# Query rows preset by GpSimd instead of ScalarE, query-gate taps as a piece of their own, and maxima in other places around the last experts

## The chip, the cores and the metric

One core of a Trainium2 chip runs the whole program in one launch. The metric is the device time in microseconds (us) from launch to end. The engines are named as the profile names them: PE (TensorE) multiplies, DVE (VectorE) and ACT (ScalarE) work on whole tiles, POOL is GpSimd, and SP only issues DMA transfers here. Each engine runs its own list of instructions in order, and waits on semaphores for the others.

## The reference, cut to what matters

2048 tokens of 128 features pass through four blocks, each added to the residual `x` behind a layer norm.

```
x = x + selective_scan_block(layernorm(x))            # 64 time chunks of 32
x = x + shared_and_8_routed_experts(layernorm(x))     # hidden 512, silu, top 2 of 8
x = x + attention(layernorm(x)):
    q, k = conv3(x), conv3(x) projected;  v = linear(x)          # 16 heads of 8
    tau   = sigmoid(conv1(gelu(depthwise_conv3(x, tau1))))       # one per head and query
    delta = sigmoid(conv1(gelu(depthwise_conv3(x, del1))))       # one per head and key
    scores = (q . k) / sqrt(8) * tau[query] + delta[key]
    x += linear(softmax(scores) @ v)
x = x + hashed_experts(layernorm(x))                  # each token to 2 of 8
```

## The kernel before, in words

The tokens are worked in four chunks of 512. While the scan runs, the routed experts of chunk *tc* run interleaved, and for the last chunk (*tc* = 3) they run by themselves from 642.8 us, in a stretch that also prepares the attention of chunks 0 to 2. The function `scan_order` is called once by every engine, and each engine passes it generators that issue its own part of each named stage; `scan_order` pulls pieces of them in one common order. So moving a call in `scan_order` moves instructions on all engines together.

The experts of a chunk are 9 (one shared, eight routed) times four hidden tiles: 36 *ups* (L631, two matmuls into a hidden tile that ACT turns into `HB` at L1050) and 36 *downs* (L622, two matmuls that sum into one PSUM bank). After an expert's last down, DVE weighs the sum by the token's gate (L1364, `GO`), and the first down of a later expert must wait for that (`gated`); POOL adds it up (L1683). At the end PE turns the sum round (L645), DVE adds it to `x_tok` (L1378), and the layer norm of chunk 3 starts (L1209).

The attention of chunk *c* is prepared by these pieces. `kside`: depthwise taps of the delta gate (DVE, L1425 and L1429), key convolution (PE, L695, `w_convk`), the split of keys into three bf16 parts (DVE L1407 to L1415, `k_parts`), gate product (PE L706, `d2w`), the delta parts on POOL (L1702 to L1710). `qside`: taps of the tau gate (for chunks 0 to 2 on POOL, L1736 to L1742; for chunk 3 on DVE), query convolution (L695, `w_convq`), values (PE L742, DVE L1458), gate product (L706, `t2w`), sigmoid on ACT (L1095), times tau and the split of queries (DVE L1464, then L1407 to L1415, `q_parts`). SP writes the parts to DRAM scratch `sc` (L1905 keys, L1917 delta, L1931 queries) and reads them back as rows: L1912 (12 transfers, keys) and L1922 (6, delta) into the key buffer `KS`, L1896 (12, queries) into `QP`. The rows of query chunk 0 are read when the query parts of chunk 1 are in DRAM.

A score is a product of key rows and query rows. Rows 48 to 50 and 112 to 114 of `QP` meet the three parts of delta, and must be 1. `QP` has two slots; each is filled before its first use, by ACT at L1137, from a column `tmpl` that POOL made at the program's start.

Before the exponentials of a group of heads, the largest score of each query is taken: a pair of matmuls fills two PSUM banks, one DVE reduction of 1024 columns reads them into `mx`. Those of the first head group are split: 16 *early* ones (keys of chunks 0 and 1; PE L779, DVE L1476) run among the last experts, one per scheduling step from step 36 on; 17 *firsts* (keys of chunks 2 and 3; PE L797, DVE L1491) run while chunk 3's attention is prepared; and `AHEAD` = 10 of the second head group (PE L812, DVE L1500) run there too. Then the maxima are reduced (L1487), turned (PE L835), split, and sent through DRAM into `QP`; after that the first score (PE L843) can start the attention proper.

Of the kernel before, what the change touches and what calls it, by code (L numbers as in the profile page):

```python
# [17 lines left out]
NS = 64  # L18
# [56 lines left out]
def scan_order(p):  # L75
# [3 lines left out]
    K0 = p["kside"](0)  # L79
    lgen = chain(some(K0, 4), beside(K0, p["qside"](0)), beside(p["kside"](1), p["qside"](1)), p["later"](2),  # L80
                 beside(p["kside"](2), p["qside"](2)))
    for k in range(-2, NS + 1):
# [36 lines left out]
        if k == NS:  # L119
            lgen = pull(lgen, 2)  # L120
        if 0 <= k - 1 < NS:
# [12 lines left out]
    L, K, Q = p["later"](3), p["kside"](3), p["qside"](3)  # L134
    m = Slots()
# [61 lines left out]
def nothing(*_):  # L197
    pass


PROLOG, NORM, EPILOG, GATES, FFN, COMBINE, KSIDE, QSIDE = 35, 5, 12, 12, 41, 12, 8, 7

IDLE = dict(prolog=lambda tc: idle(PROLOG), epilog=lambda tc: idle(EPILOG), gates=lambda tc: idle(GATES),
            ffn=lambda tc: idle(FFN), later=lambda tc: idle(NORM), combine=lambda: idle(COMBINE), start=nothing,
            kside=lambda c: idle(KSIDE), qside=lambda c: idle(QSIDE), early=nothing, first=nothing, ahead=nothing,
            rows=nothing, mulW=nothing, mulB=nothing, scanX=nothing, scanP=nothing, mulC=nothing, clamp=nothing,
# [127 lines left out]
def build(nc, A, out):  # L334
    with ExitStack() as ctx:
# [595 lines left out]
        def scalar_program(e):  # L931
# [184 lines left out]
            def qside(c):  # L1116
                a, b = RANGE[c]
                yield
                w.wait_ge(S("mm_convq"), c + 1)
                w.wait_ge(S("q_parts"), 5 * c)  # L1120
                conv(c, 0, 0, 1, "conv_q")
                yield
                for g in range(2):
                    if c < 3:
                        w.wait_ge(S("t2"), 10 * c + 5 * g + 5)
                    else:
                        w.wait_ge(S("t1"), 24 + 3 * g + 3)
# [12 lines left out]
                yield  # L1140
                yield
# [54 lines left out]
        def vector_program(e):  # L1196
# [219 lines left out]

            def taps(c, i, g, base):

                a, b = RANGE[c]
                t = TC[2 * i + g][:, 0:b - a]  # L1420
# [4 lines left out]
                e.tensor_scalar(t, xnT[:, a:b], t1w[:, i, g, 0:1], t1w[:, i, g, 3:4], ALU.mult, ALU.add).then_inc(  # L1425
                    S("t1"), 1)
# [18 lines left out]
            def qside(c):  # L1445
                a, b = RANGE[c]
                n = b - a
                if c == 3:
                    w.wait_ge(S("mm_gate_t"), 3)
                    taps(c, 0, 0, 24)  # L1450
                yield
                if c == 3:
                    taps(c, 0, 1, 27)
                yield
                w.wait_ge(S("mm_v"), c + 1)
# [148 lines left out]
        def gpsimd_program(e):  # L1604
# [11 lines left out]

            e.memset(tmpl[:, :], 0.0).then_inc(S("tmpl"), 1)
            for n, p in enumerate((48, 49, 50, 112, 113, 114)):
                w.wait_ge(S("tmpl"), n + 1)
                e.affine_select(out=tmpl[:, :], in_=tmpl[:, :], compare_op=ALU.not_equal, fill=1.0, base=-p,  # L1620
                                pattern=[[0, 1]], channel_multiplier=1).then_inc(S("tmpl"), 1)

            def power(i, st, pre):
# [99 lines left out]

            def qside(c):
                a, b = RANGE[c]
                n = b - a

                def taps(g):
# [23 lines left out]
                if c < 3:
                    taps(1)
                yield
                yield from idle(5)
# [50 lines left out]
        def sync_program(e):  # L1806
# [239 lines left out]
```

## Time and profile before

| | us |
|---|---|
| device time, median of 3 (lowest, highest) | 1692.63 (1691.33, 1693.41) |
| profiled execution, its device time | 1693.37 |
| its span, first to last instruction | 1691.5 |
| last experts: L601 to L645 | 642.80 to 771.27 |
| chunk 3's attention inputs: L645 to L835 | 771.27 to 833.72 |
| first score, L843 | 841.66 |

The mean granted TensorE clock is 0.912. A profile row gives when an instruction (or a run of one form) starts, how long it takes, and in brackets how long its engine stood idle before it and what ended that.

### The profile page before, as it was taken

What the parts mean: (1) busy time and instruction counts of PE and PEld (TensorE: products, weight loads), DVE (VectorE), ACT (ScalarE), POOL (GpSimd) and SP (SyncE); (2) the same over time, 40 slices, a digit from 0 to 9 for tenths busy, and PEclk for the clock granted to TensorE, in tenths of its full rate; (3) what the DMA queues carried; (4) which work ended last, traced back from release to release, by engine and by line L of the source; (5) the groups of instructions that cost most, each with busy time, mean ns of one, the idle gap of its engine ahead of it and who ended that gap; (6) DMA issues with size and microseconds to landing.
All of it is one profiled execution on the core that took longest, in us unless ns stands there. A gap on an engine that the chain in (4) does not pass through costs nothing.

```text
span 1691.5 us, 21904 instructions
## 1 busy us (share of the span) xinstructions
PE 1414.6 (84%) x8188; PEld 515.5 (30%) x8188; DVE 1250.6 (74%) x1498; ACT 1069.8 (63%) x1770; POOL 595.4 (35%) x534
## 2 busy tenths in 40 slices
PE   3445779678966987886499999999999999999998
PEld 1111234233432433332122222222222222344443
DVE  1799888887899783566799999999999994022222
ACT  3532467457725736533189989998999899743433
POOL 0678757865876765452020010001110100000000
PEclk9675789888977988997599999999999999999999
DMA  8122222212222202341112001000100000011110
GB/s 227 38 70 75 64 69 75 69 57 69 87 62 76 81 25 59 62 68 26 40 24 49 27 2 21 2 3 2 21 3 2 2 3 2 26 38 50 44 45 24
DMA packets 57566, 75.59 MB, mean 45 GB/s; under 512 B 7090, under 2 KB 29747, under 8 KB 57459
## 3 DMA queue, kind: packets, MB, share of 16 engines
q1 hardware_dynamic: 57458, 74.18, 16.7%
q8 instruction: 64, 1.05, 0.3%
q14 instruction: 44, 0.35, 0.1%
HBM read 69.18 MB, written 4.98 MB: 44 GB/s over the span
## 4 chain that ended last, share of the span: by engine, by line
PE 51%; DVE 27%; POOL 8%; issue 8%; ACT 4%; DMA 0%; SPq 0%; DVEq 0%; POOLq 0%; ACTq 0%
DVE mx L1500 14%; PE PS L855 11%; PE PS L905 7%; PE PS L917 7%; PE PS L843 6%; PE PS L622 4%; PE PS L812 4%; PE PS L631 4%; POOL D L1655 3%; DVE D L1283 3%; DVE PS L1269 2%; POOL D L1662 2%; DVE PS L1275 2%; PE PS L579 2%; PE PS L547 2%
## 5 line engine op out<-in xcount | busy, mean ns | idle before, releaser
L1168 ACT ACTIVATE aa<-PS 128x512 f32<-128x512 f32 x1024 | 551.3, 598 | 51.0 <-PE PS L843 41.0
L1500 DVE TENSOR_REDUCE mx<-PS 128x2 f32<-128x1024 f32 x480 | 552.2, 1219 | 14.6 <-PE PS L812 11.5
L855 PE MATMUL PS<-aa,D 128*32 128x256 f32 x4096 | 321.6, 391 | 1.6 <-ACT aa L1168 0.6
L843 PE MATMUL PS<-D 54*128 54x512 bf16 x1024 | 212.1, 390 | 15.9 <-ACT aa L1168 8.9
L579 PE MATMUL PS<-D,ident 128*128 128x512 f32 x256 | 155.2, 741 | 64.1 <-POOL D L1662 56.5
L812 PE MATMUL PS<-D 51*128 51x512 bf16 x960 | 190.7, 386 | 17.9 <-DVE mx L1500 16.0
L1766 POOL CAST n<-nm 4x512 bf16<-4x512 f32 x15 | 9.1, 605 | 483.4 <-ACT nm L1150 483.4
L1662 POOL TENSOR_TENSOR D<-D 128x1024 f32<-128x1024 f32 x64 | 150.8, 2356 | 72.2 <-DVE D L1283 72.2
L1189 ACT ACTIVATE D<-PS,h_b 128x512 f32<-128x512 f32 x128 | 88.1, 688 | 130.5 <-PE PS L905 130.5
L1023 ACT ACTIVATE D<-D,Am 128x512 f32<-128x512 f32 x128 | 85.3, 715 | 129.3 <-DVE D L1283 127.4
L1269 DVE TENSOR_TENSOR_SCAN PS<-PS,D 128x512 f32<-128x512 f32 x128 | 157.6, 1231 | 11.3 <-POOL D L1671 3.5
L1655 POOL TENSOR_TENSOR D<-D 128x1024 f32<-128x1024 f32 x64 | 150.6, 2352 | 42.1 <-PE PS L579 37.6
L631 PE MATMUL PS<-xnT,f_w 128*128 128x512 f32 x288 | 152.4, 629 | 13.2 <-ACT HB L1050 13.2
L1050 ACT ACTIVATE HB<-PS 128x512 f32<-128x512 f32 x144 | 85.2, 597 | 107.8 <-PE PS L631 107.4
L622 PE MATMUL PS<-HB,f_w 128*128 128x512 f32 x288 | 150.5, 629 | 1.8 <-ACT FO L1054 1.3
L1588 DVE SCALAR_TENSOR_TENSOR aa<-PS,h_b,aa 128x512 f32<-128x512 f32 x32 | 24.0, 751 | 171.3 <-PE PS L917 171.3
L855 PEld LDWEIGHTS PS<-aa,D 128*32 128x32 f32 x4096 | 84.2, 108 | 194.8 <-issue 154.6
L905 PE MATMUL PS<-xnT,aa 128*128 128x512 f32 x256 | 130.8, 593 | 0.0
L1283 DVE TENSOR_TENSOR_SCAN D<-D,hl,PS 128x512 f32<-128x512 f32 x96 | 122.5, 1276 | 1.9
L843 PEld LDWEIGHTS PS<-D 54*128 54x128 bf16 x1024 | 53.6, 93 | 226.6 <-ACT aa L1168 161.5
L917 PE MATMUL PS<-D 128*128 128x512 f32 x224 | 114.3, 592 | 0.0
L579 PEld LDWEIGHTS PS<-D,ident 128*128 128x128 f32 x256 | 56.9, 235 | 145.7 <-POOL D L1662 74.5
(271 smaller groups left out, 1563.8 us busy)
## 6 DMA issues: line engine op xcount, KB each, us to landing
D<-bc SPq DMA_DIRECT2D x128, 256.0 KB, 3.4
GB<-gd SPq DMA_DIRECT2D x32, 256.0 KB, 3.9
aa<-gh SPq DMA_DIRECT2D x32, 256.0 KB, 3.3
D<-sc SPq DMA_DIRECT2D x72, 64.0 KB
f_w<-in_L_ffn_experts_w SPq DMA_DIRECT2D x1, 2048.0 KB, 9.1
f_w<-in_L_ffn_experts_w SPq DMA_DIRECT2D x8, 256.0 KB, 5.9
aa<-in_L_ffn_W SPq DMA_DIRECT2D x8, 256.0 KB, 3.8
D<-in_L_ffn_W SPq DMA_DIRECT2D x7, 256.0 KB, 4.1
```

What stands on the lines that cost most here:

```text
L579: e.matmul(bank(g), ident[:, :], wb[k % 3][:, g, :], start=(n == 0), stop=(n == 15)).then_inc(S("mm_sum"), 1)
L622: e.matmul(bank(SUM_BANK[tc]), f_w2[:, n // 4, n % 4, :], HB1[i % 6], start=(n % 4 == 0), stop=(n % 4 == 3)).then_inc(S("mm_down"), 1)
L631: e.matmul(bank(4 + i % 2), f_w1[:, n // 4, 128 * (n % 4):128 * (n % 4) + 128], XN[:, ts], start=True, stop=True).then_inc(S("mm_up"), 1)
L812: t = e.matmul(to[:, hh, :], query(hh, qc % 2, p, b), KS[64 * hh:64 * hh + 51, p, 512 * c:512 * c + 512], start=True, stop=True)
L843: e.matmul(take_exp(s + hh), KS[64 * hh:64 * hh + 54, p, 128 * kb:128 * kb + 128], QP[64 * hh:64 * hh + 54, qc % 2, p, :], start=True, sto ...
L855: t = e.matmul(PS[32 * j:32 * j + 32, 7, cs], va[:, kb, 9 * h:9 * h + 32], Pt[K % 3][:, 512 * j + 256 * n:512 * j + 256 * n + 256], start= ...
L905: e.matmul(to, hw1[x % 8][:, 128 * j:128 * j + 128], XN[:, 512 * q:512 * q + 512], start=True, stop=True).then_inc(S("e_full"), 1)
L917: e.matmul(bank(4 + 2 * (x % 2)), hw2[x % 8][:, 128 * j:128 * j + 128], HB3[d % 8], start=(j == 0), stop=(j == 3)).then_inc(S("x_full"), 1)
L1168: e.activation(Pt[K % 3][:, c:c + 512], bank((s + hh) % 3), ACT.Exp).then_inc(S("e_free"), 1)
L1269: e.tensor_tensor_scan(out=bank(3), data0=bank(2), data1=ab[k % 3][:, g, :], initial=0.0, op0=ALU.max, op1=ALU.mult).then_inc(S("sP"), 1)
L1500: e.tensor_reduce(mx4[:, G % 2, b, 2 * pair:2 * pair + 2, c:c + 1], max_banks(m), AX.X, ALU.max).then_inc(freed(m)[0], 1)
L1655: e.tensor_tensor(wb[k % 3], DU[tc % 2][:, :, :], Bb[k % 3].unsqueeze(1).to_broadcast([128, 2, C]), ALU.mult).then_inc(S("wB"), 1)
```

## The change

It has four parts. (1) `QP`'s rows are set to 1 by a POOL memset of the whole slot (128x2048 words of 32 bits) in POOL's `qside`, for chunks 0 and 1; ACT's two fills and the `tmpl` column are gone. (2) The tau gate's taps become a stage `tside` of two pieces, which is on POOL for all four chunks, so DVE's taps of chunk 3 are gone; chunk 3's taps on POOL wait for the key parts. (3) In `scan_order`, `made_beside` puts the pieces of chunks 0 to 2 in another order and at other steps; the early maxima stand at steps 33 to 37, 40 to 43 and 46 to 52 instead of 36 to 51. (4) The order behind the last experts is another, and `AHEAD` is 6 instead of 10: four maxima of the second group now come behind the reduction of the first.

```diff
-    lgen = chain(some(K0, 4), beside(K0, p["qside"](0)), beside(p["kside"](1), p["qside"](1)), p["later"](2),
-                 beside(p["kside"](2), p["qside"](2)))
+    lgen = made_beside(p, K0)
...
     for step, _ in enumerate(chain(p["epilog"](3), both(p["gates"](3), p["ffn"](3)))):
-        if step in (1, 2, 10, 13) or step >= 16:
+        if step in (1, 2, 10, 13):
+            pull(K0)
+        elif step == 8:
+            drain(p["tside"](0))
+        elif step >= 16:
             lgen = pull(lgen)
-        if 0 <= step - EARLY_FROM < EARLY:
-            p["early"](step - EARLY_FROM)
+        if step in EARLY_STEPS:
+            p["early"](EARLY_STEPS.index(step))
...
     pull(K, 4)
+    pull(tau)
+    firsts(3)
+    pull(K, 2)
+    drain(tau)
+    firsts(4)
     pull(Q)
-    pull(K)
-    pull(Q)
-    firsts(3)
-    pull(K)
-    firsts(4)
-    pull(K)
-    pull(Q)
-    firsts(5)
-    pull(Q)
-    firsts(6)
+    firsts(5, 6)
     drain(K)
     pull(Q)
     firsts(7)
-    ahead(0, 1)
     pull(Q)
-    ahead(2, 3)
+    ahead(*range(AHEAD))
+    firsts(8, 9, 10)
+    pull(Q, 2)
+    firsts(11, 12)
     drain(Q)
-    ahead(*range(4, AHEAD))
-    firsts(*range(8, 17))
+    firsts(*range(13, 17))
+
+
+def made_beside(p, K0):
+
+    Q, tau = p["qside"](0), p["tside"](1)
+    yield from beside(K0, some(Q, 4))
+    yield from beside(tau, Q)
+    yield from beside(p["kside"](1), p["qside"](1))
+    yield from p["later"](2)
+    yield from beside(p["kside"](2), chain(p["tside"](2), idle(1), p["qside"](2)))
...
-EARLY, EARLY_FROM = 16, 36
-AHEAD = 10
+EARLY_STEPS = (33, 34, 35, 36, 37, 40, 41, 42, 43, 46, 47, 48, 49, 50, 51, 52)
+AHEAD = 6
...
                 w.wait_ge(S("q_tau"), c)
                 gate(c, tauC, 128, cols[:, 6:7], 1, 0, "gate_t")
-                if c < 2:
-                    w.wait_ge(S("tmpl"), 7)
-                    w.wait_ge(S("mm_sum"), 2 * NS)
-                    e.activation(QP[:, c, :, :], tmpl[:, :].unsqueeze(2).to_broadcast([128, 8, 512]),
-                                 ACT.Copy).then_inc(S("q_tmpl"), 1)
...
-                if c == 3:
-                    w.wait_ge(S("mm_gate_t"), 3)
-                    taps(c, 0, 0, 24)
...
+                    if c == 3:
+                        w.wait_ge(S("k_parts"), 20)
...
+                if c < 2:
+                    e.memset(QP[:, c, :, :].bitcast(mybir.dt.uint32), 0x3F803F80).then_inc(S("q_ones"), 1)
```

Three places of it. The first is PE among the last experts, in two pieces that begin at the same down product (the fourth of expert 4, counted from 0). In the kernel before, L622 is a down, L631 an up, L508 a transpose for chunk 2's norm, L695 the convolutions of chunk 2, L742 its values, L779 the early maximum:

```order
L622 MATMUL PS<-HB,f_w 128x512
L508 MATMUL PS<-ident,xn 128x128 [waits gate_t,p_xn]
L508 MATMUL PS<-ident,xn 128x128 x3
L631 MATMUL PS<-xnT,f_w 128x512 [waits hid]
L695 MATMUL PS<-xnT,w_convk 128x512 [waits gate_d,p_ln]
L695 MATMUL PS<-xnT,w_convk 128x512 x2
L695 MATMUL PS<-xnT,w_convq 128x512 x3
L631 MATMUL PS<-xnT,f_w 128x512 [waits hid]
L622 MATMUL PS<-HB,f_w 128x512 [waits gated]
L622 MATMUL PS<-HB,f_w 128x512
L742 MATMUL PS<-w_Wv,xnT 128x128 x4
L631 MATMUL PS<-xnT,f_w 128x512 [waits hid]
```
Behind these stands one more L622, and then the first L779. In the changed kernel the same down is L632, an up is L641, and the early maximum is L789:

```order
L632 MATMUL PS<-HB,f_w 128x512
L789 MATMUL PS<-D 128x511 [waits d_key1,d_key0,d_q0]
L789 MATMUL PS<-D 128x511
L641 MATMUL PS<-xnT,f_w 128x512 [waits hid]
L789 MATMUL PS<-D 128x512 [waits f_free]
L789 MATMUL PS<-D 128x512
L641 MATMUL PS<-xnT,f_w 128x512 [waits hid]
L632 MATMUL PS<-HB,f_w 128x512 [waits gated]
L632 MATMUL PS<-HB,f_w 128x512
L518 MATMUL PS<-ident,xn 128x128 [waits gate_t,p_xn]
L518 MATMUL PS<-ident,xn 128x128 x3
L789 MATMUL PS<-D 128x511 [waits f_free]
```

The first early maximum now stands directly behind that down; the transpose, the two convolutions, the values, three ups and three downs of the list before stand behind it, and its wait is the same.

The second is DVE behind the query parts of chunk 0, also among the last experts. Before, with L1364 the weighing of expert 1 and L1425, L1429 the delta taps of chunk 1:

```order
L1411 CAST D<-D 128x511 [waits q_parts]
L1413 TENSOR_TENSOR D<-D 128x511 [waits q_parts]
L1415 CAST D<-D 128x511 [waits q_parts]
L1425 TENSOR_SCALAR D<-xnT,t1w 128x512 [waits p_ln,mm_gate_d]
L1429 SCALAR_TENSOR_TENSOR D<-xnT,t1w,D 128x512 [waits t1] x2
L1364 SCALAR_TENSOR_TENSOR GO<-PS,GB 128x512 [waits ffn_sum,d_G0,mm_down]
```

Now, where L1366 is the weighing:

```order
L1413 CAST D<-D 128x511 [waits q_parts]
L1415 TENSOR_TENSOR D<-D 128x511 [waits q_parts]
L1417 CAST D<-D 128x511 [waits q_parts]
L1366 SCALAR_TENSOR_TENSOR GO<-PS,GB 128x512 [waits ffn_sum,d_G0,mm_down]
L1427 TENSOR_SCALAR D<-xnT,t1w 128x512 [waits p_ln,mm_gate_d]
L1431 SCALAR_TENSOR_TENSOR D<-xnT,t1w,D 128x512 [waits t1] x2
```

The weighing moved ahead of the taps, and stays behind the parts.

The third is DVE behind the key parts of chunk 3. Before, L1425 and L1429 are the tau taps of chunk 3, L1491 firsts, L1500 maxima ahead:

```order
L1425 TENSOR_SCALAR D<-xnT,t1w 128x513 [waits mm_gate_t]
L1429 SCALAR_TENSOR_TENSOR D<-xnT,t1w,D 128x513 [waits t1] x2
L1425 TENSOR_SCALAR D<-xnT,t1w 128x513
L1429 SCALAR_TENSOR_TENSOR D<-xnT,t1w,D 128x513 [waits t1] x2
L1491 TENSOR_REDUCE mx<-PS 128x2 [waits m_full] x2
L1458 TENSOR_TENSOR D<-PS,bb 128x16x8 [waits va,mm_v]
L1458 TENSOR_TENSOR D<-PS,bb 128x16x8 x3
L1491 TENSOR_REDUCE mx<-PS 128x2 [waits m_full] x3
L1500 TENSOR_REDUCE mx<-PS 128x2 [waits m_full] x2
L1464 SCALAR_TENSOR_TENSOR D<-D 128x513 [waits gate_t,conv_q]
L1407 CAST D<-D 128x513 [waits d_sq,q_tau]
L1409 TENSOR_TENSOR D<-D 128x513 [waits q_parts]
```

Now, L1487 firsts, L1496 maxima ahead, L1454 values, L1460 to L1417 the query parts:

```order
L1487 TENSOR_REDUCE mx<-PS 128x2 [waits m_full] x5
L1454 TENSOR_TENSOR D<-PS,bb 128x16x8 [waits va,mm_v]
L1454 TENSOR_TENSOR D<-PS,bb 128x16x8 x3
L1496 TENSOR_REDUCE mx<-PS 128x2 [waits m_full] x6
L1487 TENSOR_REDUCE mx<-PS 128x2 [waits m_full] x5
L1460 SCALAR_TENSOR_TENSOR D<-D 128x513 [waits gate_t,conv_q]
L1409 CAST D<-D 128x513 [waits d_sq,q_tau]
L1411 TENSOR_TENSOR D<-D 128x513 [waits q_parts]
L1413 CAST D<-D 128x513 [waits q_parts]
L1415 TENSOR_TENSOR D<-D 128x513 [waits q_parts]
L1417 CAST D<-D 128x513 [waits q_parts]
L1487 TENSOR_REDUCE mx<-PS 128x2 [waits m_full] x3
```

The taps are gone from it. Ahead of the values stand 5 maxima instead of 2, between them and the query parts 11 instead of 5, behind the parts 3 instead of 16: in all 19 instead of 23. On PE the gate product `t2w` of chunk 3, which stood behind the pair for the 3rd of these maxima, now stands behind the pair for the 14th, and three of that 14 wait for `d_key3`.

## Rows read from the trace of the kernel before

**Rows 1.** The page's first part: busy us, share of the span and instructions of each engine.

```profile
PE 1414.6 (84%) x8188; PEld 515.5 (30%) x8188; DVE 1250.6 (74%) x1498; ACT 1069.8 (63%) x1770; POOL 595.4 (35%) x534
```

**Rows 2.** Windows by stage: busy us, instructions; granted TensorE clock, DMA share, GB/s.

```profile
642.80:771.27 128.47, 107.38 (x263) 43.55 (x263) 69.49 (x103) 64.18 (x84) 66.62 (x59) 0.91 0.33 57
771.27:833.72 62.45, 33.67 (x128) 12.07 (x129) 49.17 (x68) 13.04 (x21) 7.67 (x9) 0.64 0.14 27
700.00:708.00 8.00, 5.70 (x8) 2.42 (x9) 3.40 (x7) 3.58 (x6) 1.62 (x2) 0.57 0.66 82
708.00:727.00 19.00, 19.00 (x54) 8.72 (x52) 12.89 (x18) 7.75 (x16) 12.46 (x12) 1.00 0.60 96
```

**Rows 3.** Groups of PE's instructions by line, 708 to 727 us: busy, mean ns, idle.

```profile
L622 PE MATMUL PS<-HB,f_w 128*128 128x512 f32 x16 | 7.8, 592 | 0.0
L631 PE MATMUL PS<-xnT,f_w 128*128 128x512 f32 x14 | 7.0, 592 | 0.0
L695 PE MATMUL PS<-xnT,w_convk 128*128 128x512 f32 x6 | 2.8, 608 | 0.0
```

**Rows 4.** Timeline of PE, 664 to 716 us: start, duration, idle before.

```profile
673.85 2.07 PE L631 MATMUL PS<-xnT,f_w 128*128 128x512 f32 x2 [3.72 <-ACT HB L1050]
...
690.79 1.99 PE L706 MATMUL PS<-D,t2w 128*128 128x512 f32 x4 [0.53 <-DVE D L1458]
...
702.30 2.07 PE L631 MATMUL PS<-xnT,f_w 128*128 128x512 f32 x2 [4.37 <-ACT HB L1050]
...
714.39 1.02 PE L622 MATMUL PS<-HB,f_w 128*128 128x512 f32 x2
```

**Rows 5.** By source line (L1137, L1411, L1716; L1931's landing): duration ns min/median/max, starts.

```profile
L1137 ACT ACTIVATE D<-tmpl x2: 3599/3603/3607, 668.3 to 696.7; 128x4096 bf16<-128x4096 f32 x2
...
L1411 DVE CAST D<-D x8: 430/664/3037, 633.7 to 813.4; 128x512 bf16<-128x512 f32 x4, 128x511 bf16<-128x511 f32 x2, 128x513 bf16<-128x513 f32 x2
...
L1716 POOL MEMSET D<- x4: 1805/1805/1809, 630.6 to 777.9; 128x2048 uint32 x4
...
DMA to landing us min/median/max: 2.6/5.1/7.9
```

**Rows 6.** Timeline of DVE, 664 to 704 us.

```profile
677.28 0.69 DVE L1364 SCALAR_TENSOR_TENSOR GO<-PS,GB 128x512 f32<-128x512 f32 x1 [1.98 <-PE PS L622]
...
696.94 0.73 DVE L1464 SCALAR_TENSOR_TENSOR D<-D 128x512 f32<-128x512 f32 x1 [1.72 <-ACT D L1095]
```

**Rows 7.** Timeline of SP's DMA issues, 700 to 727 us.

```profile
702.72 0.39 SPq L1931 DMA_DIRECT2D sc<-D  x1
710.59 4.10 SPq L1896 DMA_DIRECT2D D<-sc  x12
...
715.13 3.84 SPq L1922 DMA_DIRECT2D D<-sc  x6
```

**Rows 8.** Window of 2 us, in which the last early rows land.

```profile
726.00:728.00 2.00, 2.00 (x7) 0.65 (x6) 1.93 (x3) 1.66 (x2) 1.91 (x2) 1.00 0.21 56
```

**Rows 9.** Timeline of PE, 726 to 768 us: first early maximum, last down products.

```profile
727.07 0.39 PE L779 MATMUL PS<-D 51*128 51x511 bf16 x2
...
765.61 1.98 PE L622 MATMUL PS<-HB,f_w 128*128 128x512 f32 x4
```

**Rows 10.** Timeline of DVE, 770 to 834 us.

```profile
775.33 0.86 DVE L1209 BATCH_NORM_STATS2 st<-x_tok 128x6 f32<-128x128 f32 x4
...
801.03 2.36 DVE L1491 TENSOR_REDUCE mx<-PS 128x2 f32<-128x1024 f32 x2 [6.04 <-PE PS L797]
...
823.96 9.14 DVE L1491 TENSOR_REDUCE mx<-PS 128x2 f32<-128x1024 f32 x8
```

**Rows 11.** Timeline of PE, 786 to 842 us.

```profile
790.59 3.60 PE L706 MATMUL PS<-D,d2w 128*16 128x512 f32 x4 [3.40 <-ACT D L1107]
...
804.23 1.99 PE L706 MATMUL PS<-D,t2w 128*128 128x512 f32 x4 [1.53 <-DVE D L1458]
...
841.66 0.61 PE L843 MATMUL PS<-D 54*128 54x512 bf16 x2 [6.93 <-DMA D<-sc]
```

More of the change, by code:

```diff
@@ L119, in scan_order @@
         if k == NS:
-            lgen = pull(lgen, 2)
+            pull(K0, 2)
         if 0 <= k - 1 < NS:
@@ L128, in scan_order @@
     for step, _ in enumerate(chain(p["epilog"](3), both(p["gates"](3), p["ffn"](3)))):
-        if step in (1, 2, 10, 13) or step >= 16:
+        if step in (1, 2, 10, 13):
[3 more added lines that the diff above has]
+        elif step >= 16:
             lgen = pull(lgen)
-        if 0 <= step - EARLY_FROM < EARLY:
-            p["early"](step - EARLY_FROM)
+        if step in EARLY_STEPS:
+            p["early"](EARLY_STEPS.index(step))
     drain(lgen)
-    L, K, Q = p["later"](3), p["kside"](3), p["qside"](3)
+    L, K, tau, Q = p["later"](3), p["kside"](3), p["tside"](3), p["qside"](3)
     m = Slots()
@@ L198, in nothing @@
     pass
-PROLOG, NORM, EPILOG, GATES, FFN, COMBINE, KSIDE, QSIDE = 35, 5, 12, 12, 41, 12, 8, 7
+PROLOG, NORM, EPILOG, GATES, FFN, COMBINE, KSIDE, TSIDE, QSIDE = 35, 5, 12, 12, 41, 12, 8, 2, 7
 IDLE = dict(prolog=lambda tc: idle(PROLOG), epilog=lambda tc: idle(EPILOG), gates=lambda tc: idle(GATES),
             ffn=lambda tc: idle(FFN), later=lambda tc: idle(NORM), combine=lambda: idle(COMBINE), start=nothing,
-            kside=lambda c: idle(KSIDE), qside=lambda c: idle(QSIDE), early=nothing, first=nothing, ahead=nothing,
+            kside=lambda c: idle(KSIDE), tside=lambda c: idle(TSIDE), qside=lambda c: idle(QSIDE), early=nothing, first=nothing, ahead=nothing,
             rows=nothing, mulW=nothing, mulB=nothing, scanX=nothing, scanP=nothing, mulC=nothing, clamp=nothing,
@@ L215 @@
 LAG = 3
-EARLY, EARLY_FROM = 16, 36
-AHEAD = 10
+EARLY_STEPS = (33, 34, 35, 36, 37, 40, 41, 42, 43, 46, 47, 48, 49, 50, 51, 52)
+EARLY = len(EARLY_STEPS)
+AHEAD = 6
 FIRST = 17 + AHEAD
@@ L364, in build @@
         bb = sb("bb", [128, 2, 128])
-        tmpl = sb("tmpl", [128, 1])
         mx4 = sb("mx4", [128, 2, 4, 4, 5])
@@ L1415, in parts_of, with taps @@
                 e.tensor_copy(out_[2], src).then_inc(done, 1)
-            def taps(c, i, g, base):
+            def taps(c, g):
                 a, b = RANGE[c]
-                t = TC[2 * i + g][:, 0:b - a]
+                t, base = TC[2 + g][:, 0:b - a], 6 * c + 3 * g
                 w.wait_ge(S("mm_out"), 3)
@@ L1424, in taps @@
                 w.wait_ge(S("edge"), 2)
[L1425 removed]
+                e.tensor_scalar(t, xnT[:, a:b], t1w[:, 1, g, 0:1], t1w[:, 1, g, 3:4], ALU.mult, ALU.add).then_inc(
                     S("t1"), 1)
@@ L1434, in kside @@
                 w.wait_ge(S("mm_gate_d"), c)
-                taps(c, 1, 0, 6 * c)
+                taps(c, 0)
                 yield
-                taps(c, 1, 1, 6 * c + 3)
+                taps(c, 1)
                 yield
@@ L1447, in qside @@
                 n = b - a
-                if c == 3:
-                    w.wait_ge(S("mm_gate_t"), 3)
-                    taps(c, 0, 0, 24)
[L1451 to L1454, printed above, removed]
+                yield from idle(2)
                 w.wait_ge(S("mm_v"), c + 1)
@@ L1615, in gpsimd_program @@
             e.memset(starts[:, 0:C:32], E20).then_inc(S("const"), 1)
[L1617 to L1621, printed above, removed]
             def power(i, st, pre):
@@ L1722, in kside, with tside @@
                 yield from idle(2)
-            def qside(c):
+            def tside(c):
                 a, b = RANGE[c]
@@ L1742, in taps, with qside @@
                         e.tensor_tensor(t, t, m, ALU.add).then_inc(S("t2"), 1)
+                taps(0)
+                yield
+                taps(1)
+                yield
+            def qside(c):
                 v = va[:, 4 * c:4 * c + 4, :]
@@ L1748, in qside @@
                 e.memset(v[:, :, 0:144].rearrange("p b (h c) -> p b h c", c=9)[:, :, :, 8:9], 1.0).then_inc(S("va"), 1)
-                if c < 3:
-                    taps(0)
+                if c < 2:
+                    e.memset(QP[:, c, :, :].bitcast(mybir.dt.uint32), 0x3F803F80).then_inc(S("q_ones"), 1)
                 yield
[L1752 to L1755, printed above, removed]
+                yield from idle(6)
             scan_order(IDLE | dict(start=start, prolog=prolog, mulB=mulB, mulC=mulC, clamp=clamp, epilog=epilog, ffn=ffn, later=later,
-                                   kside=kside, qside=qside))
+                                   kside=kside, tside=tside, qside=qside))
             meet(e, w, "pool")
@@ L1890, in load_q @@
                 w.wait_ge(S("d_sq"), 16 * min(qc + 2, 4))
-                w.wait_ge(S("q_tmpl"), sl + 1)
+                w.wait_ge(S("q_ones"), sl + 1)
                 if qc >= 2:
```

7 lines of the change are left out of this document (2 added, 5 removed).

## The prediction, made before the changed kernel ran

> **What bounds the kernel now.** I read the page's first part, then the windows by stage, then the timelines of the engines that wait. PE is busy for 84% of the span, DVE for 74% [rows 1]: neither is the bound everywhere, so the change is worth what the stage is worth in which it lies. All of it lies ahead of the first score. During the last experts PE is busy for 107.38 of 128.47 us [rows 2]: PE's list sets the end there, and what counts is where it stops. It stops twice for ACT: 3.72 us before 673.85 and 4.37 us before 702.30 [rows 4], each time released by the silu of a hidden tile (L1050), because ACT was in L1137, 3.60 us each [rows 5]. After the second stop PE runs at a granted clock of 0.57 for 8 us, and at 1.00 from 708 on [rows 2]: near the lower of its two levels, 1.2 GHz, after an idle stretch, then the upper, 2.4. In the stretch behind (771.27 to 833.72) PE has 33.67 us of work and DVE 49.17 of 62.45 [rows 2], and its last 9.14 us are eight maxima back to back [rows 10]: DVE sets that end, with one hole of 6.04 us before 801.03 [rows 10], where PE is slow with chunk 3's products. From 833.72 to 841.66 little but a trip through DRAM happens: PE idles 6.93 us for it [rows 11].
>
> **The copies (gain).** Without L1137 the two stops go: 2 x 3.60. With them goes slow running: in 700 to 708 PE's busy 5.70 us at 0.57 would be 5.70 x 0.57 = 3.2, so 2.4 less; after the first stop a pair took 2.07 instead of 1.02 [rows 4] and the next one about half of that excess more, 1.6 together. Sum 11.2 us up to the down product that ends at 714.39 + 0.86 = 715.25 (the next instruction's start; 1.02 holds a drain). The POOL memset that replaces a copy takes, by the same size, 1.80 [rows 5]; POOL is busy for 66.62 of 128.47 us [rows 2], and the rows are read by SP only when the query parts of chunk 1 have landed, so I cost it at nothing; were it in front of those parts' own work it would cost 1.8. Building `tmpl` at the program's start lay beside the loads: nothing.
>
> **What PE now waits for instead (loss).** I walked through the new order with the old durations. (a) The weighing of expert 1 stood between taps on DVE and ran at 677.28 [rows 6]; it still stands behind the query parts of chunk 0, which now begin later, since chunk 0's tau product moved back by several products. I get these parts from 671.4 to 676.7, the weighing to 677.5, while PE asks for it at 674.2: 3.3 us. (b) The delta product of chunk 1 is reached 1.6 us before its input. (c) The weighing of expert 3 costs 2.4 us behind the query parts of chunk 1. So PE ends the down of 715.25 at 715.25 - 11.2 + 7.3 = 711.3, some 4 us earlier.
>
> **The first early maximum (the term that decides).** It now stands directly behind that down. Before, the transposes, two convolutions, the values, three ups and three downs stood between, and it ran at 727.07 without idle time [rows 9]. It waits for the rows of query chunk 0, which SP reads when the query parts of chunk 1 lie in DRAM. Before: t2w of chunk 1 at 690.79 [rows 4], parts from 696.94 [rows 6], write issued at 702.72, 12 reads from 710.59, 6 delta reads from 715.13 to 719 [rows 7]; in 726 to 728 the DMA share is down to 0.21 from 0.60 before 727 [rows 2, 8], and the last of these rows lands at 726.9, just in time. None of this chain got shorter but for ACT's copy, which stood behind the sigmoids and so delayed nothing in it. The convolutions of chunk 1 come two downs later, and t2w of chunk 1 ends 1.7 us later by my walk; the parts are done at 704.2 instead of 702.7. From there 24.2 us (702.72 to 726.9) give 728.4; if the write lands in the median of 5.1 us instead of 7.9 [rows 5], 725.6. I take 726.5. PE, there at 711.3, idles for 15 us.
>
> **From there to the norm.** Left on PE are 14 ups, 16 downs, 13 early pairs, the transposes, two convolutions, the values and two gate products. A 512-column product is worth 0.43: in 708 to 727 PE never idles, and 16 + 14 + 12 of them with the short ones fill 19.00 us [rows 2, 3]. So 60 x 0.43 = 25.8, early pairs 13 x 0.32 = 4.2, convolutions 5.2, gates 3.4, the rest 1.3: 39.9. Add slow running after so long a stop, 2.9 (the 2.4 above or a little more), and two shorter waits of my walk, 3.1 (expert 5's gate) and 2.6 (t2w of chunk 2). The last down ends at 726.5 + 39.9 + 2.9 + 5.7 = 775.0, before at 767.53 (765.61 + 1.92) [rows 9]. From there the norm of chunk 3 began 7.8 us later, at 775.33 [rows 10]; now two more early maxima stand on DVE in that tail, 1.0 each net: 9.8. So the norm begins at 784.8: **+9.5**.
>
> **Behind the last experts.** Before, from the norm to 833.72 (L835): 58.4. Up to the key parts nothing changes (15.6). Behind them DVE has 19 maxima at 1.13 (9.14 / 8 [rows 10]) = 21.5, the values 0.9, query parts 3.5, small ones 1.0: 26.9. Holes: the delta product d2w, 3.60 at low clock from 790.59 [rows 11], delays the first maximum by 4.2; the query convolution (3.8) makes a hole of 3.4; key rows of chunk 3 0.8; and t2w, now between two maxima pairs, 3.2, if the clock is low then as it was at d2w (at 804.23 it took 1.99 [rows 11]; then 1.5). 15.6 + 26.9 + 11.6 = 54.1: **-4.3**. Taking the taps from DVE is worth nothing by itself: they filled the hole that ended at 801.03. Most of it is the four maxima, 4.5, which now lie in the gap behind L835. There the fourth's pair stands ahead of the score on PE, and its buffer comes free some 7 us behind L835, when the score could start: 0 to 0.6.
>
> The Trainium skill, "SBUF — State Buffer", section "SBUF: two separate sides", says that VectorE and GpSimd share one pair of ports under an exclusive lock, so that one instruction fully blocks the other. The rows agree in one place: of eight casts at L1411, which take 0.43 us at least and 0.66 in the median, one took 3.04 [rows 5], and it lay beside a POOL memset of 1.80. By that rule new memsets can delay parts; what it would give here is rival 3.
>
> **Sum.** Against the profiled execution's 1693.37 (span 1691.5 and 1.9 around it): +9.5 - 4.3 + 0.3 = 1698.9. The profiled execution is 0.7 above the median of 1692.63, so 1698.2; I shade it to **1697.8**, since a row can land earlier but not much later.
>
> **Rivals.** A measurement of this kernel tells 0.2% (3.4 us) from no change.
> 1. The rows come early enough, so it is faster. The point from which it decides: the sum is zero when they land at 726.5 - 5.5 = 721. For it: a write of this kind landed in 2.6 us at best [rows 5], which from 728.4 gives 723; for more, t2w of chunk 1 must come earlier too. Faster by 0.2% needs 718. With no stop at all (711.3) 15 us of idling and 2.9 of slow running go: 1680. Against it: t2w comes later, not earlier. 0.17.
> 2. Rows at 719 to 723, or a t2w of chunk 3 at full clock: within 0.2%, about 1693. 0.24.
> 3. As forecast, and a new memset on POOL meets a cast of the query parts on DVE, as one met a cast before (3.04 - 0.43 = 2.6 us [rows 5]), or the clock falls in the stops of 3.3 and 3.1 us (it fell after 3.72 us before [rows 4], costing 1.6): 2 to 5 us more, 1701. What delays the parts of chunk 1 delays the landing in full. 0.12.
> 4. The forecast, 1694 to 1700. 0.47.
>
> **How the numbers follow.** Range 1687 to 1703: above it only both mishaps of rival 3, below it rival 1 with landing before 717. Faster 0.17, same 0.24, slower 0.59.
>
> **What would show it.** In the changed trace: L1137 gone and no stop of PE for L1050 near 673 and 702; a weighing at 677 with PE idle for about 3 us; PE idle for 12 to 16 us in front of the first early maximum (L789), which starts between 724 and 729, with the granted clock near 0.5 behind it; L645 at about 778 and the norm (L1211) at 785; from there to L845 about 54 us, with holes on DVE at d2w, w_convq and t2w; the first score 8 us behind. I am wrong if L789 finds its rows landed; then the walk misjudged either PE's arrival or the transfers.

## The result, and the profile after

| | before | changed |
|---|---|---|
| device time, median (lowest, highest), 4 runs each | 1693.02 (1691.33, 1694.06) | 1704.87 (1702.15, 1708.03) |
| profiled execution, its span | 1693.37, 1691.5 | 1708.03, 1706.2 |
| last experts, gate logits to fold (L601 to L645; now L611 to L655) | 128.47 | 139.32 |
| fold to the norm of chunk 3 (L1209; L1211) | 4.06 | 6.22 |
| norm to the turn of the maxima (L835; L845) | 58.39 | 58.62 |
| turn to the first score (L843; L853) | 7.94 | 7.98 |
| all behind it | 849.84 | 849.96 |

The change makes the kernel slower: ratio 1.0072, 95% interval 1.0052 to 1.0091, some 12 us. The profiled execution is the slowest of the four and 14.7 us of span above that of before: 10.9 among the last experts, 2.2 in the tail to the norm, 0.2 in the stretch behind, and 1.3 ahead of all this, where the scan still runs (over the twelve kernels of this study the last experts start anywhere from 640.68 to 644.10 us, and at 642.23 in experiment 4, which is the same program up to there, so this part is scatter).

The windows of the changed kernel, first the last experts, then norm to turn; the columns are those of [rows 2]:

```profile
644.10:783.42 139.32, 109.43 (x260) 43.77 (x261) 66.20 (x102) 62.88 (x86) 70.79 (x62) 0.88 0.26 51
789.64:848.26 58.62, 31.88 (x112) 12.09 (x113) 37.95 (x56) 13.14 (x21) 19.86 (x19) 0.62 0.15 29
679.00:683.00 4.00, 4.00 (x5) 1.84 (x6) 3.89 (x5) 0.00 (x0) 3.79 (x3) 0.50 0.60 164
728.00:732.00 4.00, 4.00 (x8) 1.41 (x7) 3.11 (x4) 1.92 (x5) 1.26 (x1) 0.50 0.10 36
746.00:750.00 4.00, 3.80 (x5) 1.14 (x6) 3.90 (x5) 2.29 (x3) 3.82 (x4) 0.57 0.00 0
```

The last three rows are short pieces of the first window, in which the granted clock is 0.50, 0.50 and 0.57. PE has nearly the same work as before in the first window, which is 10.9 us longer, at 0.88 of full clock instead of 0.91. PE's timeline among the last experts shows where:

```profile
679.00 3.78 PE L632 MATMUL PS<-HB,f_w 128*128 128x512 f32 x4 [3.31 <-DVE GO L1366]
682.57 3.93 PE L705 MATMUL PS<-xnT,w_convk 128*128 128x512 f32 x6
...
695.69 1.89 PE L716 MATMUL PS<-D,d2w 128*16 128x512 f32 x4 [1.43 <-ACT D L1117]
...
710.03 1.98 PE L632 MATMUL PS<-HB,f_w 128*128 128x512 f32 x4 [2.53 <-DVE GO L1366]
...
714.43 1.02 PE L632 MATMUL PS<-HB,f_w 128*128 128x512 f32 x2
727.43 0.61 PE L789 MATMUL PS<-D 51*128 51x511 bf16 x2 [11.98 <-DMA D<-sc]
727.97 2.07 PE L641 MATMUL PS<-xnT,f_w 128*128 128x512 f32 x2
...
746.20 3.63 PE L632 MATMUL PS<-HB,f_w 128*128 128x512 f32 x4 [2.03 <-DVE GO L1366]
...
762.96 3.26 PE L716 MATMUL PS<-D,t2w 128*128 128x512 f32 x4 [2.30 <-issue]
...
783.42 0.63 PE L655 MATMUL PS<-ident,FO 128*128 128x128 f32 x4 [1.63 <-POOL FO L1673]
```

The two stops for the silu behind a copy [rows 4] are gone, and so is L1137. In their place stand a stop of 3.31 us for a weighing of DVE (`GO`), 1.43 for chunk 1's delta gate, 2.53 for a weighing, and 11.98 us for the rows of the first early maximum (L789), which is released by a DMA. In these 11.98 us no instruction of DVE, ACT or POOL runs either. Behind the first of the four stops, four downs take 3.78 us (1.88 at full clock) and the key convolution 3.93 (2.74); behind the fourth, a pair takes 2.07. SP's DMA issues show the chain that L789 waits for, as [rows 7] before:

```profile
709.41 0.39 SPq L1926 DMA_DIRECT2D sc<-D  x1
712.48 4.10 SPq L1891 DMA_DIRECT2D D<-sc  x12
716.62 3.84 SPq L1917 DMA_DIRECT2D D<-sc  x6
```

The write of the query parts (L1926) is issued at 709.41 instead of 702.72, and 18.0 us later L789 starts: the first read is issued 3.1 us behind the write, SP issues the 18 reads one behind the other until 720.46, and 7.0 us more pass before L789 starts. In the stretch behind, DVE's timeline has a hole that before did not have:

```profile
789.64 0.86 DVE L1211 BATCH_NORM_STATS2 st<-x_tok 128x6 f32<-128x128 f32 x4
...
809.53 2.36 DVE L1487 TENSOR_REDUCE mx<-PS 128x2 f32<-128x1024 f32 x2 [3.93 <-PE PS L807]
814.29 3.49 DVE L1487 TENSOR_REDUCE mx<-PS 128x2 f32<-128x1024 f32 x3 [2.40 <-PE PS L807]
824.03 0.88 DVE L1454 TENSOR_TENSOR D<-PS,bb 128x128 f32<-128x128 f32 x4 [6.25 <-POOL D L1746]
...
838.43 2.36 DVE L1487 TENSOR_REDUCE mx<-PS 128x2 f32<-128x1024 f32 x2 [3.34 <-PE PS L807]
```

The values of chunk 3 (L1454) start after 6.25 us of idling, released by POOL's L1746. POOL's timeline shows what it did until then: it waited for the key parts (L1417), then worked through the first piece of the taps, the parts of delta and the second piece of the taps, five operations a piece, and only then through the two memsets of the values' buffer.

```profile
805.81 0.77 POOL L1728 TENSOR_SCALAR D<-xnT,t1w 128x513 f32<-128x513 f32 x1 [11.80 <-DVE D L1417]
...
812.25 0.61 POOL L1692 CAST D<-D 16x513 bf16<-16x513 f32 x1
...
816.60 0.76 POOL L1728 TENSOR_SCALAR D<-xnT,t1w 128x513 f32<-128x513 f32 x1
...
821.97 1.09 POOL L1734 TENSOR_TENSOR D<-D 128x513 f32<-128x513 f32 x1
823.00 0.66 POOL L1744 MEMSET D<- 128x672 f32 x1
823.72 0.21 POOL L1746 MEMSET D<- 128x64 f32 x1
```

In the kernel before, where chunk 3's tau taps were on DVE, POOL set this buffer long before DVE wrote the values at 803.30:

```profile
779.63 0.67 POOL L1746 MEMSET D<- 128x672 f32 x1
780.35 0.21 POOL L1748 MEMSET D<- 128x64 f32 x1
```

In the changed kernel PE is stopped behind DVE, since both buffers of the maxima are full; the last hole of DVE above, 3.34 us, stands behind the gate product `t2w` at 3.78 us:

```profile
826.10 0.60 PE L822 MATMUL PS<-D 51*128 51x512 bf16 x2 [7.88 <-DVE mx L1496]
...
833.43 3.78 PE L716 MATMUL PS<-D,t2w 128*128 128x512 f32 x4
...
848.26 1.01 PE L845 MATMUL PS<-ident,mxh 128*4 128x128 f32 x4 [1.32 <-DVEq L486]
...
856.24 0.61 PE L853 MATMUL PS<-D 54*128 54x512 bf16 x2 [0.47 <-DMA D<-sc]
```

### The profile page after: what moved, and what is told of

It reads as the page before. It is cut to its first block, busy times and chain, and to the rows that moved or that the text cites. A ratio compares the mean times of both kernels' runs of the same rounds, so it can differ in the third digit from the quotient of the medians.

```text
span 1706.2 us, 21900 instructions
## 1 busy us (share of the span) xinstructions
PE 1421.0 (83%) x8188; PEld 516.1 (30%) x8188; DVE 1244.7 (73%) x1492; ACT 1067.7 (63%) x1772; POOL 610.7 (36%) x539
## 3 DMA queue, kind: packets, MB, share of 16 engines
q1 hardware_dynamic: 57458, 74.18, 16.9%
## 4 chain that ended last, share of the span: by engine, by line
PE 51%; DVE 26%; POOL 10%; issue 9%; ACT 3%; DMA 1%; SPq 1%; POOLq 0%; DVEq 0%; ACTq 0%
DVE mx L1496 13%; PE PS L865 11%; PE PS L915 6%; PE PS L927 6%; PE PS L853 6%; PE PS L632 4%; PE PS L822 4%; POOL D L1645 3%; PE PS L641 3%; DVE D L1285 3%; DVE PS L1271 2%; POOL D L1652 2%; PE PS L589 2%; PE PS L557 2%; DVE PS L1277 2%
## 5 line engine op out<-in xcount | busy, mean ns | idle before, releaser
L1496 DVE TENSOR_REDUCE mx<-PS 128x2 f32<-128x1024 f32 x480 | 552.2, 1216 | 10.3 <-PE PS L822 7.1
L853 PE MATMUL PS<-D 54*128 54x512 bf16 x1024 | 212.1, 390 | 9.5 <-ACT aa L1170 8.9
L632 PE MATMUL PS<-HB,f_w 128*128 128x512 f32 x288 | 152.7, 637 | 9.1 <-DVE GO L1366 7.9
L641 PE MATMUL PS<-xnT,f_w 128*128 128x512 f32 x288 | 153.0, 633 | 6.0 <-ACT HB L1060 6.0
L853 PEld LDWEIGHTS PS<-D 54*128 54x128 bf16 x1024 | 53.6, 93 | 220.2 <-ACT aa L1170 161.6
```

The source lines that it names most:

```text
L632: e.matmul(bank(SUM_BANK[tc]), f_w2[:, n // 4, n % 4, :], HB1[i % 6], start=(n % 4 == 0), stop=(n % 4 == 3)).then_inc(S("mm_down"), 1)
L641: e.matmul(bank(4 + i % 2), f_w1[:, n // 4, 128 * (n % 4):128 * (n % 4) + 128], XN[:, ts], start=True, stop=True).then_inc(S("mm_up"), 1)
L853: e.matmul(take_exp(s + hh), KS[64 * hh:64 * hh + 54, p, 128 * kb:128 * kb + 128], QP[64 * hh:64 * hh + 54, qc % 2, p, :], start=True, sto ...
L1496: e.tensor_reduce(mx4[:, G % 2, b, 2 * pair:2 * pair + 2, c:c + 1], max_banks(m), AX.X, ALU.max).then_inc(freed(m)[0], 1)
```

## The experiments

Times are medians. Experiments 1 to 4, 5 to 8, and 9 and 10 ran on three chips, each time with the kernel before beside them (1693.44, 1693.05 and 1693.98). Single executions of one kernel lie several us apart, so the ratio to the kernel before and its interval decide. A difference between two experiments of different groups is the less certain for it. The stage times are those of one profiled execution each.

| kernel | us | ratio, 95% interval | last experts | tail | norm to turn | stop for the first rows |
|---|---|---|---|---|---|---|
| before | 1693.02 | 1 | 128.47 | 4.06 | 58.39 | none |
| changed | 1704.87 | 1.0072 (1.0052, 1.0091) | 139.32 | 6.22 | 58.62 | 11.98 |
| 1 changed, values' buffer first | 1698.31 | 1.0036 (1.0021, 1.0051) | 136.37 | 6.68 | 51.32 | 12.68 |
| 2 changed, taps on DVE | 1699.41 | 1.0032 (1.0018, 1.0046) | 139.27 | 6.22 | 54.47 | 11.96 |
| 3 before, preset alone | 1685.41 | 0.9948 (0.9932, 0.9964) | 117.55 | 4.07 | 61.21 | none |
| 4 changed, early maxima at 37 to 52 | 1691.75 | 0.9992 (0.9983, 1.0002) | 123.30 | 6.68 | 57.59 | none |
| 5 before, six maxima ahead | 1688.30 | 0.9973 (0.9963, 0.9982) | 128.43 | 4.07 | 53.88 | none |
| 6 both repairs of 1 and 4 | 1685.32 | 0.9954 (0.9937, 0.9970) | 123.94 | 6.68 | 54.24 | 0.93 |
| 7 as 3, early maxima at 33 to 52 | 1697.39 | 1.0020 (1.0006, 1.0035) | 128.31 | 6.00 | 60.09 | 13.42 |
| 8 order of before, then the changed one | 1680.92 | 0.9928 (0.9908, 0.9948) | 121.11 | 4.07 | 52.16 | 4.02 |
| 9 as 8, early maxima one step later | 1678.65 | 0.9907 (0.9890, 0.9924) | 117.64 | 6.00 | 53.88 | none |
| 10 as 6, query pieces one step later | 1686.87 | 0.9961 (0.9940, 0.9981) | 125.34 | 6.00 | 52.46 | 1.45 |

**1. The values' buffer ahead of the taps.** In POOL's list for chunk 3:

```diff
             def tside(c):
+                if c == 3:
+                    ones_of_v(c)          # the two memsets of va, moved out of qside
                 taps(0)
```

> The changed kernel, with the memset of chunk 3's values buffer moved ahead of chunk 3's tau taps on GpSimd. In the changed kernel VectorE stood idle for 6.25 us until GpSimd had set that buffer. Theory A (only this wait cost time there): about 6 us less than the changed kernel's 1704.9, so 1699. Theory B (the taps on GpSimd also hold up the delta parts, so that key rows of chunk 3, read from 821.9 on and landed some 7 us later, are late next): the maxima of chunk 3's keys, which would be reached near 824, wait until about 828, and 2 to 3 us are left of the gain, 1702.

Norm to turn fell by 7.3 us, to 51.32, and the time by 6.6: theory A, on the upper side. The DVE hole at the values is gone, and no late key rows took its place. Its trace also serves as a control on the clock:

```profile
726.95 0.61 PE L789 MATMUL PS<-D 51*128 51x511 bf16 x2 [12.68 <-DMA D<-sc]
...
745.37 1.98 PE L632 MATMUL PS<-HB,f_w 128*128 128x512 f32 x4 [2.03 <-DVE GO L1366]
...
760.47 1.96 PE L716 MATMUL PS<-D,t2w 128*128 128x512 f32 x4 [2.30 <-issue]
```

The downs behind the stop of 2.03 us, 3.63 us in the changed kernel, take 1.98 here (granted clock 1.00 from 745 to 749), and the gate product 1.96 instead of 3.26: the same stops, with the clock fallen in one execution and not in the other. It is 3.6 us of the distance from L789 to the fold: 55.99 us with PE busy for 48.70 in the changed kernel, 52.39 with 45.09 here, and 7.3 of idling in both. In experiment 2, where this stage is the same too, the clock fell as in the changed kernel (3.63 and 3.26).

**2. Chunk 3's taps on DVE again**, all else as changed:

```diff
+            def tside(c):                 # DVE; GpSimd's tside passes chunk 3 by
+                if c == 3:
+                    w.wait_ge(S("mm_gate_t"), 3)
+                    taps(c, 0, 0, 24)
```

> The changed kernel, with chunk 3's tau taps back on VectorE, all else as changed. Theory B (GpSimd's taps cost twice, by the values buffer and by late key rows): from the norm of chunk 3 to the turn of the maxima 51 to 54 us instead of 58.6, and 5 to 7 us less than the changed kernel, 1698 to 1700. Rival: the taps' 4.2 us on VectorE come on top of the maxima, and nothing is gained, 1704.

54.47 us from norm to turn and 5.5 us less in all: the wait for the buffer is what the taps on POOL cost, for without them it is gone too. Whether the taps are better on POOL or on DVE once the buffer is first is not shown: the window is 51.32 us in experiment 1 and 54.47 here, but 54.24 in experiment 6, which has this stage as in 1, and the ratios of experiments 1 and 2 can't be told apart.

**3. The preset alone.** The kernel before with ScalarE's copies and `tmpl` out and

```diff
                 if c < 3:
                     taps(1)
+                if c < 2:
+                    e.memset(QP[:, c, :, :].bitcast(mybir.dt.uint32), 0x3F803F80).then_inc(S("q_ones"), 1)
```

> The kernel before, with only the first part of the change: GpSimd presets the query rows, ScalarE's two copies and the column they read are gone. Theory A (the early maxima, not the copies, set the pace from there on): TensorE reaches the first early maximum near 716 instead of 727, and its rows land near 722, since the first copy lay ahead of their chain and the second did not; 5 us are won there, 2 of them lost to a low clock, 1688 to 1690. Rival (what two copies cost is won in full): 11 us less, 1682.

Both theories missed the total, the rival was nearer in the mechanism. PE found the rows there when it came, 73.3 us behind the gate logits instead of 84.3:

```profile
714.74 0.39 PE L778 MATMUL PS<-D 51*128 51x511 bf16 x2
```

```profile
696.08 0.39 SPq L1921 DMA_DIRECT2D sc<-D  x1
700.51 4.11 SPq L1886 DMA_DIRECT2D D<-sc  x12
...
705.06 3.83 SPq L1912 DMA_DIRECT2D D<-sc  x6
```

The last experts are 10.9 us shorter, which is what two copies with their slow clock were put at (11.2), so nothing was lost to the landing: it took at most 18.7 us from the write's issue, not 24.2. Of this 2.8 us went again between norm and turn, where PE was busy for 35.58 us at a granted clock of 0.58; in the kernel before the same window has 32.11 at 0.65:

```profile
763.10:824.31 61.21, 35.58 (x120) 12.73 (x121) 46.20 (x66) 13.02 (x21) 7.66 (x9) 0.58 0.12 28
```

The gate product `t2w` alone took 3.78 us there instead of 1.99 [rows 11]. So the total is 8 us.

**4. The early maxima later, in the changed kernel.**

```diff
-EARLY_STEPS = (33, 34, 35, 36, 37, 40, 41, 42, 43, 46, 47, 48, 49, 50, 51, 52)
+EARLY_STEPS = tuple(range(37, 53))
```

> The changed kernel, with the 16 early maxima at steps 37 to 52, so that the first stands four steps later. Theory A (the stop of 12 us at the first early maximum and the low clock behind it are what the last experts lost): TensorE comes there as the rows land, the stop is 0 to 3 us, and 10 to 14 us less than the changed kernel, 1691 to 1695. Rival (TensorE waits elsewhere instead, for the gates of experts behind a dense run of maxima on VectorE): 1700 or more.

13.1 us less: theory A. L789 starts at 723.34 with no stop, and the last experts take 123.30 instead of 139.32. (That is 16.0 us; the changed kernel's profiled execution is 3.2 us above its median, this one 2.4 below.)

**5. Six maxima ahead, in the kernel before** (`AHEAD = 6`).

> The kernel before, with AHEAD at 6 instead of 10 and nothing else. Theory A (the four maxima lay on VectorE's path at 1.13 us each, and behind the turn of the maxima they fit into the gap of 8 us): 4 us less than the kernel before, 1689. Rival (they come back one for one, in the gap or in the attention): 1693.

4.7 us less, 4.5 of it between norm and turn (53.88); the gap behind is 7.95, as before. Theory A.

**6. Both repairs of the changed kernel.**

> The changed kernel, with the values buffer set ahead of the tau taps and the early maxima at steps 37 to 52. Theory A (the two losses lie in different stages and add up): 7 us less than with the later early maxima alone (1691.7), so 1685. Rival (the two meet in one limit, such as the landing of chunk 3's key rows): 1689 or more.

1685.32, where the two gains add to 1704.9 - 6.6 - 13.1 = 1685.2. The window norm to turn is 54.24 instead of 51.32 here: PE stops for 4.31 us for the key rows of chunk 3, for which it did not stop in experiment 1 (see 9).

**7. Only the early maxima moved, in experiment 3's kernel**, to the changed kernel's steps.

> The kernel before with GpSimd's preset alone (1685.4), and the early maxima at the changed kernel's steps 33 to 52. Theory A (rows land some 18 us behind the issue of the query parts' write, at 714, and TensorE is there at 704): a stop of about 10 us in front of the first early maximum, a low clock behind it, and 8 to 12 us more than without, 1693 to 1697. Rival (the stop is taken back, since the work of chunk 2 lies behind it and less is left at the end): 1686 to 1689.

12.0 us more than without it (ratio 1.0020 instead of 0.9948), and the stop is back, in the order of before:

```profile
718.41 0.61 PE L779 MATMUL PS<-D 51*128 51x511 bf16 x2 [13.42 <-DMA D<-sc]
```

The work that was moved behind the first early maximum does not give it back.

**8. The order of before, then the changed one.** `made_beside` gives way to

```diff
-    lgen = made_beside(p, K0)
+    lgen = chain(some(K0, 4), beside(K0, made_q(p, 0)), beside(p["kside"](1), made_q(p, 1)), p["later"](2),
+                 beside(p["kside"](2), made_q(p, 2)))          # made_q: beside(tside(c), qside(c))
...
-EARLY_STEPS = (33, 34, 35, 36, 37, 40, 41, 42, 43, 46, 47, 48, 49, 50, 51, 52)
+EARLY_STEPS = tuple(range(36, 52))
```

and from chunk 3 on it is experiment 1. On POOL the preset stands one piece later than in the changed kernel, which is its place in experiment 3.

> The order of before among the last experts (early maxima at 36 to 51, the pieces of chunks 0 to 2 as before), with GpSimd's preset, and behind the last experts the changed order with six maxima ahead, chunk 3's tau taps on GpSimd, and the values buffer set ahead of them. Theory A (each stage keeps what it showed by itself: last experts 117.6 us, from the norm to the turn of the maxima 51.3 instead of 58.4): 7 us less than the preset alone, 1678. Rival (as with the changed kernel's order, one of the two depends on the other): 1682 or more.

1680.92, faster than both kernels, between the two theories: the window norm to turn kept its gain (52.16), but this time the rows were 4.02 us late for PE in the profiled execution, and the last experts took 121.11 instead of 117.55.

**9. The same with the early maxima at 37 to 52.**

> The fastest so far (1680.9), with the early maxima one step later, 37 to 52. There TensorE still stopped for 4.02 us for the first rows. Theory A (landing sets it): the stop shrinks to 2 or less, and 1 to 3 us less. Rival (one more early maximum falls behind the last expert and lengthens the tail of 4.07 us to the norm by 1 to 2.6, as with the changed order, where it was 6.7): same or up to 2 us more.

1678.65, 2.3 us less, but the intervals of the two ratios overlap, and the two profiled executions are equal (1679.64 and 1679.56). In the stages the stop is gone (last experts 3.5 less), the tail grew by 1.9 and norm to turn by 1.7, so both theories had a part and a gain in all is not shown. In its trace the next late thing shows, the key rows of chunk 3:

```profile
803.01 1.04 PE L799 MATMUL PS<-D 51*128 51x512 bf16 x4 [4.36 <-DMA D<-sc]
```

Experiments 6 and 9 differ in one thing, the order of the pieces of chunks 0 to 2. It is worth 6.3 us among the last experts (123.94 against 117.64), and 6.7 in the time: in experiment 6 PE waits for 3.29, 1.43 and 2.54 us ahead of the first early maximum, where 9 has one wait of 2.03 and none other over 1 us.

**10. The weighing of expert 1 ahead of the query parts**, in experiment 6's kernel:

```diff
     yield from beside(K0, some(Q, 4))
+    yield                                  # all pieces behind it one step later
     yield from beside(tau, Q)
```

> The changed order with both repairs (values buffer first, early maxima at 37 to 52; 1685.3), and one empty piece more ahead of the query pieces, so that VectorE weighs expert 1 ahead of the query parts of chunk 0 and not behind them. Theory A (the order on VectorE makes TensorE's stop of 3.3 us near 677, and that stop makes its low clock near 680): both go, some 3 + 3 us there, 2 of it lost since all query pieces come a step later; 3 to 5 us less than 1685.3. Rival (the silu or the gates stop TensorE there anyway): 1685 or more.

No gain (1686.87). The local part of theory A was right: the stop near 677 and the slow clock behind it are gone, and the gate product of chunk 1 starts at 689.26 instead of 694.28 in experiment 6. But the piece that was moved past one weighing now stands ahead of another:

```profile
677.33 2.74 PE L706 MATMUL PS<-xnT,w_convk 128*128 128x512 f32 x6
...
689.26 1.89 PE L717 MATMUL PS<-D,d2w 128*16 128x512 f32 x4 [0.24 <-ACT D L1118]
...
705.01 3.50 PE L633 MATMUL PS<-HB,f_w 128*128 128x512 f32 x4 [3.39 <-DVE GO L1367]
```

3.39 us for the weighing of expert 3, with four downs at 3.50, and 1.72 us for a silu at 700.50 took most of it: the first early maximum starts 79.9 us behind the gate logits instead of 82.1. The rest goes behind it, where PE waits for 2.99 us for a buffer of the maxima before 756.76 (1.74 in experiment 6) and four downs then take 3.62. So the sum of theory A was wrong, and the rival named other waits than those that came.

## Why the prediction was right and wrong

The sign and the mechanism of the main loss were right, the size was not: 1697.8 was forecast, with 1703 as the upper end, and 1704.9 came. Two steps failed. "Taking the taps from DVE is worth nothing by itself" put at nothing a wait of 6.25 us for a buffer on POOL (norm to turn: -4.3 forecast, +0.2 measured), and "slow running 2.9" left out the clock behind two short stops (the norm 3.5 us later than forecast).

**The copies.** Put at 11.2 us; experiment 3 gives 10.9 among the last experts. Right, though 2.8 of it went again between norm and turn, which the forecast did not have. The memset at no cost: right.

**The three waits in their place.** 3.3, 1.6 and 2.4 forecast; 3.31, 1.43 and 2.53 measured. What I left out of the sum, and had only as rival 3, is the clock behind the first: four downs 3.78 instead of 1.88 and a convolution 3.93 instead of 2.74, 3.1 us. With it PE is at the first early maximum at 715.3 and not 711.3 (1.3 of that is the later start).

**The landing.** 726.5 forecast, 727.43 measured, but by luck: two errors cancel. The parts were written at 709.41, 5 us later than I walked to (the same slow clock, and the later start). And from there it took 18.0 us, not the 22.3 that 726.5 supposes (24.2 as before): in the kernel before the write alone took 7.9 us, until the reads began [rows 7], and 3.1 in the changed one. That the rows landed at 726.9 before was not in the trace either: L779 did not idle, so they were there by 727.07 at the latest. In experiment 3 at most 14.2 us passed from the first read's issue to PE's start, which from 710.59 would be 724.8 (an estimate). Where PE waited for the rows, the chain took 16.9 us (experiment 6), 18.0, 18.7 (1), 20.7 (7) and 22.6 (8). The stop was therefore 11.98 us and not 15, but L789 starts 83.3 us behind the gate logits, where I had 83.7: this part of the sum held. That the early maxima's place causes the stop, and what it is worth, experiments 4 (-13.1) and 7 (+12.0) show from both sides.

**From the first early maximum to the fold.** I had 52.2 us (726.5 to 775.0 and 3.7 more); experiment 1 has 52.39, the changed kernel 55.99. That experiment 1 meets the forecast is partly luck: the two shorter waits were put at 5.7 and took 4.33, and the work was put as much too low. The 3.6 us between the two kernels are the clock, fallen behind the stops before 746.20 and 762.96. The tail grew by 2.16, forecast 2.0. So the norm is 13.0 us later, not 9.5, and the 3.5 too much arise here: the failed term is "slow running 2.9", which counted the long stop and not the two short ones behind it.

**Norm to turn.** Forecast -4.3, measured +0.2. This step failed outright. I costed "the taps leave DVE" at nothing and looked at what DVE and PE wait for, but not at what was queued behind the taps on POOL: the two memsets of the values' buffer, which the values on DVE need (`va`). Before, those taps were on DVE and the memsets done at 780.56. Experiment 1 puts this at 7.3 us in the window and 6.6 in the time. The rest of the term was nearly right: the four maxima were put at 4.5 and are 4.5 in the window of experiment 5 (4.7 of the time), and the other holes of DVE were put at 4.2, 3.4 and 3.2 and are 3.93, 2.40 and 3.34. "Key rows 0.8" was 0 (changed kernel) to 4.36 (9), so the window of a repaired kernel is 51.32 to 54.24.

**The gap behind the turn.** Forecast 0 to 0.6, measured 0.04.

**The sum.** The profiled execution is 9.1 us above the 1698.9 of the sum: 3.5 us up to the norm, 4.5 from there to the turn (58.62 where 54.1 was forecast), and the 1.3 us ahead of the last experts, less some tenths.

**The port rule.** The Trainium skill ("SBUF — State Buffer", "SBUF: two separate sides") let me expect that a new memset blocks a cast. In the changed kernel the presets ran at 659.02 and 685.96, where DVE was idle until 662.65 and 691.18, so nothing was there to block. The two presets cost nothing, and what the rule would have added, 2.6 us for a cast on the way to the landing, did not come. The 2.6 us were also too much for a memset: in the kernel before the cast of 3.04 us had begun at 685.71, when a tap sum ran on POOL, and the memset began at 686.66 and took 1.80. No run here tests the rule itself.

Rival 1 did not come for lack of early rows; rival 3's clock part did, together with a buffer that I had not in view. The range was too narrow upward: the 5.2 us above the forecast that I allowed were for the clock and the port alone, with nothing for a wait that I had missed. The result is 7.1 us above the forecast, and the wait for the buffer alone is 6.6 by experiment 1; the clock behind the two short stops is not in every execution.

## What to carry to other kernels

When a piece of work moves to another engine, list what stands behind it in that engine's queue and who waits for that; two memsets of under 1 us cost 7. An operation that waits for a long chain of transfers belongs where PE arrives after the rows have landed, with a margin for the spread of the landing: four steps of placement were worth 13 us. And price each stop of PE of 2 to 3 us with the slow clock that can follow it (3.1 us behind the stop of 3.31).

## What the runs showed of the hardware that I had not expected

The same stop can cost the clock or not. Behind a stop of 2.03 us (2.30 for the gate product) in front of the same instruction, PE ran at half speed in the changed kernel (four downs 3.63) and at full speed in experiment 1 (1.98), with nothing different in that stage but the execution; in experiment 2 it was half speed again. What decides it stays open. Nor is the changed kernel's spread, 5.9 us over four executions, a sign of this by itself: 25 executions of the kernel before, beside experiments 5 to 8, lie 8.9 us apart. And the same chain of one write and eighteen reads took from 16.9 us (experiment 6) to 22.6 (experiment 8). The write's landing took 3.1 and 6.3 of it, SP's issuing of the reads 8.0 and 8.4, and the rest, from the last issue to PE's start, 5.8 and 7.9; what made the write and the reads slower was not taken apart.
